# Three key chunks of a group-weighted attention stage computed ahead of its loop, and narrower waits before the first two probability buffers

## The reference

```python
q = _split_heads(query @ wq_k + wq_b, H)
k = _split_heads(key_in @ wk_k + wk_b, H)
v = _split_heads(value @ wv_k + wv_b, H)
logits = jnp.einsum('bhqd,bhkd->bhqk', q, k) / jnp.sqrt(jnp.asarray(dh, q.dtype))
neg = (1.0 - mask.astype(q.dtype)) * -1000000000.0
attn = jax.nn.softmax(logits + neg[:, None, :, :], axis=-1)
attn = attn * group_prob[:, None, :, :]
out = jnp.einsum('bhqk,bhkd->bhqd', attn, v)
out = out.transpose(0, 2, 1, 3).reshape(query.shape[0], -1, H * dh)
return out @ wo_k + wo_b
```

## Time and profile before

| | |
|---|---|
| median of 3 runs | 1640.19 us (1639.62 to 1642.39) |
| profiled execution | 1644.55 us, its span 1643.3 us |
| busy share | TensorE 94%, VectorE 67%, ScalarE 56%, GpSimd 29% |
| mean granted TensorE clock | 0.986 |
| the touched stage | about 828 to 1145 us of the span |

### The profile page before, as it was taken

One profiled execution on the slowest core, in us unless ns is written; L12 is line 12 of the kernel. 1 busy time (PEld: TensorE's weight loads), 2 busy tenths in 40 slices (PEclk: granted clock), 3 DMA queues, 4 the chain that ended last, 5 costly groups with the idle time before them and its releaser, 6 DMA issues.

```text
span 1643.3 us, 23163 instructions
## 1 busy us (share of the span) xinstructions
PE 1546.0 (94%) x7817; PEld 853.3 (52%) x7819; DVE 1099.1 (67%) x2244; ACT 924.2 (56%) x1764; POOL 482.4 (29%) x567
## 2 busy tenths in 40 slices
PE   8999998999998999999979999999988989999998
PEld 3477754457873444444435555555344444555536
DVE  7766764866457888889468888886477435655525
ACT  5432443553345878788457778876325645555613
POOL 0221500130001555554015656555020103333300
PEclk9999999999999999999979999999998999999999
DMA  6000210020010000001263211110174020000000
GB/s 247 1 1 13 84 52 0 39 78 1 26 46 0 20 10 11 12 9 30 102 232 101 88 30 44 45 30 20 46 194 137 25 86 21 24 12 12 1 0 26
DMA packets 40044, 80.45 MB, mean 49 GB/s; under 512 B 4539, under 2 KB 25531, under 8 KB 38235
## 3 DMA queue, kind: packets, MB, share of 16 engines
q1 hardware_dynamic: 39926, 78.97, 14.8%
HBM read 62.08 MB, written 16.78 MB: 48 GB/s over the span
## 4 chain that ended last, share of the span: by engine, by line
PE 73%; DVE 12%; issue 6%; ACT 6%; DMA 1%; PEldq 1%; POOL 1%; SPq 1%; PEld 0%; DVEq 0%; POOLq 0%; ACTq 0%
PE ps L2618 6%; PE ps L2222 3%; PE ps L2176 3%; PE ps L2200 3%; PE ps L3537 3%; PE ps L2607 3%; PE ps L3502 3%; PE ps L3512 3%; PE ps L240 3%; PE ps L3557 3%; PE ps L2629 2%; PE ps L2186 2%; PE ps L3530 2%; PE ps L3570 2%; PE ps L2218 2%
## 5 line engine op out<-in xcount | busy, mean ns | idle before, releaser
L2873 POOL TENSOR_TENSOR work<-work,arena_b 128x512 f32<-128x512 f32 x128 | 168.4, 1318 | 117.9 <-ACT work L2737 117.9
L2827 DVE CUSTOM_DVE_ANT_0 work<-ps,arena_a 128x1024 f32<-128x1024 f32 x128 | 154.7, 1210 | 0.5 <-PE ps L2618 0.3
L2719 ACT ACTIVATE work<-work,small 128x1024 f32<-128x1024 f32 x128 | 146.8, 1147 | 4.0 <-DVE small L2827 3.9
L2618 PE MATMUL ps<-identity,work 128*128 128x128 f32 x1024 | 140.1, 279 | 7.3 <-DVE work L2839 2.8
L2618 PEld LDWEIGHTS ps<-identity,work 128*128 128x128 f32 x1024 | 116.1, 143 | 55.9 <-issue 29.5
L3719 POOL TENSOR_SCALAR ctx_keys<-ctx_keys,small 128x128 f32<-128x128 f32 (+3 forms) x128 | 66.8, 535 | 171.6 <-DVE small L3644 171.6
L2839 DVE TENSOR_TENSOR work<-ps,arena_b 128x512 f32<-128x512 f32 x128 | 87.9, 687 | 34.6 <-PE ps L2618 31.0
L2737 ACT ACTIVATE work<-ps 128x512 f32<-128x512 f32 x128 | 76.3, 596 | 60.4 <-PE ps L2618 56.2
L2607 PE MATMUL ps<-work 96*128 96x512 bf16 x256 | 79.9, 395 | 13.1 <-DVE small L2827 7.5
L3596 ACT ACTIVATE ctx_keys<-ctx_keys,small 128x128 f32<-128x128 f32 (+3 forms) x128 | 70.7, 553 | 28.6 <-DVE small L3636 28.1
L2327 DVE SCALAR_TENSOR_TENSOR work<-work,ps 128x1024 int32<-128x1024 f32 x64 | 77.6, 1212 | 7.6 <-ACT work L2262 7.5
(11 more groups left out here) (472 smaller groups left out, 3604.9 us busy)
## 6 DMA issues: line engine op xcount, KB each, us to landing
work<-parts_k_L_xattn SPq DMA_DIRECT2D x14, 384.0 KB, 3.9
ctx_feat<-in_ctxT SPq DMA_DIRECT2D x2, 2048.0 KB, 19.4
ctx_keys<-in_ctx_keys SPq DMA_DIRECT2D x2, 2048.0 KB, 16.4
arena_a<-in_mask SPq DMA_DIRECT2D x2, 2048.0 KB, 7.8
arena_b<-in_groupT SPq DMA_DIRECT2D x2, 2048.0 KB, 8.6
head_weights<-in_w_L_xattn SPq DMA_DIRECT2D x8, 449.0 KB, 3.2
arena_a<-in_w_l_attn SPq DMA_DIRECT2D x1, 3072.0 KB, 15.1
head_weights<-in_w_L_attn SPq DMA_DIRECT2D x8, 384.0 KB, 3.0
```

What stands on the lines that cost most here:

```text
L2618: mm = pe.transpose(t_psum[z][:, kt * P:(kt + 1) * P], prob[i % NP][:, o:o + P], k.iden[:, :])
L2719: act.activation(p, p, ACT.Exp, scale=-1.0, bias=minmax[:, i % 8:i % 8 + 1], accum_out=sums[:, i % 8:i % 8 + 1]).then_inc(*exped.up())
L2827: dve.tensor_tensor_reduce(prob[i % NP], s_psum[i % NS], NEG[:, b, qt, :], -1.0, BIG * 3e8, OP.add, OP.min, minmax[:, i % 8:i % 8 + 1]).th ...
L2873: pool.tensor_tensor(p, p, GT[:, b, 4:8, qt * P:(qt + 1) * P], OP.mult).then_inc(*weighed_pool.up())
```

## The change

The first three of the six later chunks (numbers 6, 7 and 8, all keys) get their matmuls and their `keep` in the entry, right behind chunk 5, in banks 5, 4 and 6, and `rest[x][0]` for them is a place of its own in the tile `spare`. Their split into parts and their stores stay at the steps where they were. The loop keeps the chunks 9, 10 and 11 at steps 22, 26 and 30. New waits guard the banks: TensorE's first transposes wait for the `keep` of chunks 7 and 6, the first probabilities by values for that of chunk 8. Unit 0's first write to `PT[0]` waits for nine stores and the last `split_low` of the entry in place of eighteen stores; the wait for eighteen goes to unit 4, the first to write `PT[1]`.

```diff
--- before.py
+++ after.py
@@ -2492,13 +2492,16 @@
     FIRST = [("q", 0, 0), ("k", 0, 0), ("k", 0, S), ("k", 0, 2 * S), ("k", 0, 3 * S), ("q", 0, S)]
     LATER = [("k", 1, t * S) for t in range(4)] + [("q", 1, t * S) for t in range(2)]
     CHUNKS = FIRST + LATER
-    NF = len(FIRST)
+    NF, NE = len(FIRST), len(FIRST) + 3
+    EARLY = {NF + j: b for j, b in enumerate((5, 4, 6))}
     chunk_at = {10 + 4 * j: NF + j for j in range(len(LATER))}
     RING = (0, 1, 2, 4, 6, 7)
     PIECES = {"q": (range(0, 3), range(0, 2), range(0, 1)), "k": ((0, 0, 0), (1, 1), (2,))}
     count = lambda x, which: sum(ch[0] == which for ch in CHUNKS[:x])
     rest = [[view(w, (j % 3) * K + h * S, S) if j < NF else norm[0][:, h * S:(h + 1) * S] for h in range(2)]
             for j in range(len(CHUNKS))]
+    for x in EARLY:
+        rest[x][0] = k.spare[:, (x - NF) * S:(x - NF + 1) * S]
     parts = [(view(w, 3 * K + 768 * j, 768) if j < NF else k.wst[1][:, 0:768]).bitcast(BF16).rearrange(
         "p (j t) -> p j t", j=3) for j in range(len(CHUNKS))]
 
@@ -2590,8 +2593,13 @@
             chunk(pe, x, k.bank(RING[x]))
             if x == 2:
                 ln.var(pe, 1)
+        for x, bank in EARLY.items():
+            if x > NF:
+                pe.wait_ge(*plain(RING.index(bank)))
+            chunk(pe, x, k.bank(bank))
         pe.wait_ge(*plain(0))
         pe.wait_ge(*plain(4))
+        pe.wait_ge(*plain(NF - 1))
         for step in range(N + 11):
             i = step
             if i < N:
@@ -2611,6 +2619,8 @@
             if 0 <= i < N:
                 pe.wait_ge(*exped(i + 1))
                 for z in range(2):
+                    if i == 0:
+                        pe.wait_ge(*plain(NF + 1 - z))
                     if i:
                         pe.wait_ge(*(turned if z else weighed)(i))
                     for kt in range(4):
@@ -2623,6 +2633,8 @@
                 if b == 0:
                     pe.wait_ge(*picked(i // 16 * 2 + h + 1))
                 pe.wait_ge(*weighed(i + 1))
+                if i == 3:
+                    pe.wait_ge(*plain(NE - 1))
                 if h == 0 and i >= 8:
                     pe.wait_ge(*gathered(i // 8))
                 for kt in range(4):
@@ -2639,13 +2651,13 @@
                 pe.wait_ge(*gathered(g + 1))
                 if g:
                     pe.wait_ge(*put(g))
-                if step - 2 in chunk_at:
+                if chunk_at.get(step - 2, 0) >= NE:
                     pe.wait_ge(*plain(chunk_at[step - 2]))
                 for qt in range(4):
                     mm = pe.matmul(f_psum[:, qt * 2 * dh:(qt + 1) * 2 * dh], partial[g % 2][:, qt * P:(qt + 1) * P], fold,
                                    start=True, stop=True)
                 mm.then_inc(*folded.up())
-            if step in chunk_at:
+            if chunk_at.get(step, 0) >= NE:
                 x = chunk_at[step]
                 pe.wait_ge(*plain(x - 1))
                 if step >= 16:
@@ -2685,7 +2697,7 @@
             which, m, _ = CHUNKS[x]
             if which == "k":
                 act.wait_ge(*part(x + 1))
-                if x >= 3:
+                if 3 <= x < NF or x >= NE:
                     act.wait_ge(*low(x - 2 if x < NF else x))
                 act.activation(rest[x][0], ps, ACT.Identity, bias=bqk[:, 2 + m:3 + m]).then_inc(*k_plain.up())
 
@@ -2707,8 +2719,10 @@
             split(x)
             if x == 2:
                 ln.root(act, 1)
+        for x, bank in EARLY.items():
+            keep(x, k.bank(bank))
         for step in range(N + 9):
-            if step - 1 in chunk_at:
+            if chunk_at.get(step - 1, 0) >= NE:
                 keep(chunk_at[step - 1], f_psum)
             i = step - 2
             if 0 <= i < N:
@@ -2731,6 +2745,9 @@
             if 0 <= i < N:
                 act.wait_ge(*turn(2 * i + 2))
                 if i == 0:
+                    act.wait_ge(*stored(3 * 3))
+                    act.wait_ge(*low(NF))
+                if i == 4:
                     act.wait_ge(*stored(3 * NF))
                 if i >= 8:
                     act.wait_ge(*pv(i // 4 - 1))
@@ -2833,6 +2850,9 @@
                     dve.wait_ge(*group_in[b](1))
                 dve.wait_ge(*turn(2 * i + 1))
                 if i == 0:
+                    dve.wait_ge(*stored(3 * 3))
+                    dve.wait_ge(*low(NF))
+                if i == 4:
                     dve.wait_ge(*stored(3 * NF))
                 if i >= 8:
                     dve.wait_ge(*pv(i // 4 - 1))
```

## The result

The changed kernel takes 1632.9 us, median of 4 runs (1632.07 to 1634.45), against 1639.92 us (1639.62 to 1642.39) before. The ratio is 0.9949, with a 95% interval of 0.9933 to 0.9965. That is 7 to 8 us less and clear of no change; 1632.2 us was forecast. In the profiled execution the span is 1630.8 us.

A forecast was written before the change was run, and what follows sets the result against it. TensorE was taken to set the pace while chunks are in the loop, with two waits in the entry. 3.3 + 4.5 - 0.06 = 7.7, rounded up to 8, gave 1640.19 - 8.0 = 1632.2 us; 8-in-10 range 1630.0 to 1635.3.

The forecast's parts named there:

- The chunks: Loop, units 10 to 22: three chunks fewer, VectorE takes over as bound, 26.5 us for 31.0; gain 4.5 us.
- The fetch as cover: Entry: chunks 6 to 8 fit into TensorE's wait for heads 0 and 1; cost 0.06 us.
- The clock: Entry: TensorE works through the gap in which its clock fell, so the clock was taken as 1.00.
- rival C: Entry: the clock falls nevertheless, slowing scores and transposes; 0.9 to 1.3 us less gain, 1633.3 us; chance 12%.
- The wait for `second_in`: Entry, unit 8's scores: TensorE stands 1.4 us for the last fetch; unit 4's multiplication 3.3 us early instead of 4.0.
- The `pick`: Entry, VectorE: two `pick` before unit 4's maximum, whose start was moved from 857.06 to 853.7 by subtracting 3.4.
- The entry's sum: Entry: unit 4's multiplication starts at 860.9, 3.3 us early; bounds 2.8 and 4.0.
- rounding up to 8.0: Total: 7.7 rounded up to 8, because the wait for `second_in` lets ScalarE and GpSimd catch up before the groups.
- A: Loop: VectorE's wait for the high part stays, or stores come 0.5 us late; total 6.1, 1634.1 us; chance 18%.
- B: Loop: the chunks' removal isn't seen, groups keep 10.3 us; 3.3 us remain, 1636.9 us; chance 5%.
- D: Entry into loop: the clock's fall lasts, 5.5 us lost per group; slower from two groups on, about 1643.5; chance 2%.
- E: Entry and loop: `second_in` lands 1.4 us sooner and TensorE's full share comes; 4.0 + 5.2 = 9.2, 1631.0 us; chance 8%.

The follow-up runs named there:

- e3_changed_again: The changed kernel repeated without edits, for a second profile; ratio to the kernel before 0.9951.
- e7_beats_changed: Changed kernel plus seven filler matmuls in TensorE's pauses between the scores of units 1 to 4; ratio to the kernel before 0.9955.
- e10_own_part_buffers: Changed kernel with own parts buffers for chunks 6, 7 and 8, so their splits wait for no store; ratio to the kernel before 0.9958.
- e1_chunks_only: Changed kernel with the old wait for eighteen stores at unit 0, so only the early chunks; ratio to the kernel before 0.9973.
- e8: Changed kernel with a fourth key chunk (9) made in the entry too; ratio to the kernel before 0.9952.
- e9: Changed kernel with the first two `pick` moved behind unit 4's maximum, under GpSimd's first multiplication; ratio to the kernel before 0.9959.
- e6_pick_in_gap_changed: Changed kernel with the first two `pick` moved ahead of VectorE's first multiplication into `PT[0]`; ratio to the kernel before 0.9957.
- e11: Changed kernel plus chunk 9 in the entry, `pick` in VectorE's gap, four filler matmuls behind the scores of units 2 and 3; ratio to the kernel before 0.9954.

## Why the prediction was right, and where only by luck

**The chunks.** The mechanism was right: TensorE set the pace of those groups, and gave most of its share back. I took 4.5 us, with VectorE as the new bound at 26.5 us for the twelve units; they take 26.10 by TensorE's starts and 26.60 by VectorE's, where those were 31.00 and 31.64. That is 4.9 to 5.0 us, 4.89 up to unit 34. VectorE's waits for the high part (0.15, 0.34) are near the 0.1 I took, and its wait for a transpose is gone.

**The fetch as cover.** Right within 0.3 us. In the profile TensorE even waited 1.28 us behind the three chunks, 0.59 in `e3_changed_again`. In `e7_beats_changed` and `e10_own_part_buffers` it didn't wait at all: there the first scores start 6.97 and 7.20 us behind chunk 5, against 6.88 to 7.23 in the five profiles without early chunks. The fourth chunk used the cover up.

**The clock.** I took it as 1.00 and gave its fall 12%. It fell in both profiles of the changed kernel, so this step of the forecast was wrong and rival C's mechanism was there. The Trainium skill, "TensorE: Matmul & The Clock Gate", section "A second HAM failure mode: psum-queue depth-cycling", which I had set beside it, says that small pauses between groups can make the clock go to and fro. The traces agree as far as one fall and one rise, and not each time: `e1_chunks_only` kept 1.00 through the same bursts. The price was small. From unit 0's maximum to unit 0's multiplication it is 851.85 - 846.38 = 5.47 us in the changed kernel and 852.62 - 847.83 = 4.79 us in `e7_beats_changed`, where the clock stayed up: 0.7 us. In `e3`, `e8`, `e9` and `e10`, with the fall, it is 5.02 to 5.63 us, so 0.2 to 0.8 us. C had priced it at 0.9 to 1.3.

**The wait for `second_in`.** I charged 1.4 us of TensorE and 0.7 of VectorE; it was 0 in the profile shown, 0.15 in `e3_changed_again`, 1.10 with the clock kept up in `e7_beats_changed` and, in `e6_pick_in_gap_changed`, this:

```profile
858.42 0.61 PE L2615 MATMUL ps<-work 96*128 96x512 bf16 x2 [0.46 <-DMA work<-parts_k_L_xattn]
```

The step that failed is the pair of times behind the 1.4 us: the fetch at 859.8 and unit 8's scores ready at 858.4, that is 21.4 and 20.0 us behind chunk 5. The first took the late stores of one execution as the kernel's own. Where they landed 1.5 us sooner and nothing else was late, as in `e7_beats_changed`, the fetch came at 19.7 us and the scores could have started at 18.7. In the profile shown it was otherwise: there the nine stores of chunks 0 to 2 landed 3.3 us behind their last issue (2.1 before), so all that follows in SyncE's list came 1.2 us later, and the last fetch was issued at 17.17 us, only 0.34 sooner than in the earlier trace rows. It landed at 20.7 us, and the scores, late by the clock and by the later first maximum, came at 20.7 too. That the wait was 0 there is a coincidence of two delays.

**The `pick`.** I carried its 1.78 us for two over unchanged, from 855.28 to 857.06. It was 0.7 us of work and 1.1 us of standing behind GpSimd. This term I had not seen, although the same rows of VectorE and GpSimd of the kernel before side by side show it:

```profile
855.28 0.41 DVE L2769 TENSOR_TENSOR extra<-ctx_keys,head_weights 128x256 f32<-128x256 f32 x1
855.62 1.53 DVE L2769 TENSOR_TENSOR norm_parts<-ctx_keys,head_weights 128x256 f32<-128x256 f32 x1
...
855.38 1.48 POOL L2873 TENSOR_TENSOR work<-work,arena_b 128x512 f32<-128x512 f32 x1 [9.87 <-ACT work L2737]
```

**The entry's sum.** 3.3 us were forecast and 3.52 seen between the two first profiles, but out of other parts, and that is luck: the missing 1.1 us of `pick` stands against the clock's 0.7 us and against 0.9 us by which the first maxima came later in that execution (9.05 us behind chunk 5, 8.14 before), and the 0.7 us for `second_in` didn't come. Against all profiles the entry is worth less: unit 10 stands at 31.12, 27.66 and 28.96 us before, mean 29.25, and at 27.61 and 26.67 after, mean 27.14: 2.1 us. With 4.9 from the chunks that makes 7.0. So the forecast was high for the entry (3.3 for 2.1), a little low for the chunks (4.5 for 4.9), and the 0.3 us that were added by rounding up to 8.0 have no run behind them: the wait for `second_in`, which was their reason, was near 0. The total is within 1 us.

**The rivals.** A and B ask for VectorE's waits or late stores in the groups; `e10_own_part_buffers` and the distances in the table exclude them. D asks for a low clock far into the loop; it was back after 3.4 us. E's 9.2 us had its full share of TensorE but not its 4.0 us of entry, and no pair of profiles of the two kernels reached it, except the first of before against `e3_changed_again`, with 9.33.

What stays open: why the last stores of the first profile landed 1.5 us late, and which of the entry's forms is the commoner one in unprofiled runs. The times alone, which spread over 7.5 to 9 us for the kernel before in each group, don't show it. Open too is whether the early chunks have a part in the late landing of the first nine stores: it is 3.3, 3.3 and 3.0 us in the changed kernel's first profile, `e6` and `e8`, and 2.1 to 2.5 us in the other eleven, among them six kernels or repeats with early chunks. And why the clock held in `e1_chunks_only`.

## What to carry to other kernels

Work that only feeds something much later belongs into a wait that nothing else fills; what it's worth is its time on the pacing engine, and here the twelve units of the loop gave back 5.0 us of the 5.2 that the chunks took, to 0.02 us the same in every profile. A stall that a DMA ends should be read from more than one execution before it is priced: here it was 1.6, 2.0 and 3.4 us in the same kernel. And a VectorE instruction that is several times longer than its like has to be read beside GpSimd's timeline.

## What the runs showed of the hardware that I had not expected

- A 128x256 f32 instruction of VectorE with two SBUF inputs takes 0.42 us, and 1.05, 1.50, 1.51 and 1.53 us when it is issued 0.24 to 0.52 us behind the start of GpSimd's 1.3 us multiplication. VectorE's multiplications with a PSUM input (L2859, 0.69 us) don't show it.
- The granted clock fell from 2.4 to 1.2 GHz at about 850.2 although TensorE had no pause above 0.9 us in the three microseconds before, only short bursts, and it rose again after some 3 us of nearly unbroken work. It did so in six of the seven profiles with these bursts and without fillers; in the seventh, `e1_chunks_only`, it fell only at 854.7, behind a pause of 2.2 us. With seven and with four short filler matmuls in the pauses (`e7`, `e11`, one profile each) it stayed at 2.4 GHz.
- The same stores, in the same order, landed 2.1 to 2.4 us behind the end of the last issue in thirteen profiles and 3.7 us in one.
